# A graph layer: four PSUM banks in one instruction, in place of two and two

## The reference

```python
h = jnp.maximum(_layernorm(x, axis=-1), 0.0)
ea = edge_attr @ W_edge.T + b_edge
msg = jax.nn.relu(h[src] + ea)
aggr = jax.ops.segment_sum(msg, dst, num_segments=N_NODES)
g = (1.0 + eps) * h + aggr
g = jax.nn.relu(g @ W1.T + b1)
x = x + g @ W2.T + b2
```

## Time and profile before

| | |
|---|---|
| median of 3 runs | 1237.12 us (1236.62 to 1238.39) |
| span of the profiled execution | 1239.1 us |
| VectorE busy | 518.5 us, 42% |
| ScalarE busy | 193.0 us, 16% |
| GpSimd busy | 785.9 us, 63% |
| TensorE's matmuls | 628.9 us, 51% |

### The profile page before, as it was taken

How to read it: one execution, slowest core, us unless ns; L and a number is a source line. 1 busy time by engine, 2 the same in 40 slices (tenths; PEclk the granted TensorE clock), 3 DMA queues, 4 the chain that set the end, 5 groups by cost and what they waited for, 6 DMA issues and landing times.

```text
span 1239.1 us, 9124 instructions
## 1 busy us (share of the span) xinstructions
PE 628.9 (51%) x2786; PEld 515.6 (42%) x2786; DVE 518.5 (42%) x658; ACT 193.0 (16%) x233; POOL 785.9 (63%) x838
## 2 busy tenths in 40 slices
PE   2226544455554454555554555444555545554568
PEld 2215434344433334444444444343444434443456
DVE  6645344444433333354344333333343444333373
ACT  5102111111111111111111111111111111111114
POOL 6756666666666666666666666666666666666540
PEclk9999666665656665565665656655556565565668
DMA  8513222333222223333333332222222333232212
GB/s 217 145 33 94 66 64 67 74 85 74 67 67 67 68 67 75 72 73 75 74 93 95 76 74 66 67 67 67 64 66 68 74 88 72 68 67 61 49 29 78
DMA packets 51183, 93.30 MB, mean 75 GB/s; under 512 B 17722, under 2 KB 20443, under 8 KB 51136
## 3 DMA queue, kind: packets, MB, share of 16 engines
q0 software_dynamic: 26592, 40.85, 16.3%
q1 hardware_dynamic: 24390, 51.63, 15.2%
q10 hardware_dynamic: 154, 0.24, 0.1%
HBM read 87.85 MB, written 4.80 MB: 75 GB/s over the span
## 4 chain that ended last, share of the span: by engine, by line
another core or an unknown queue 56%; DVE 23%; issue 8%; DVEq 8%; PE 3%; DMA 1%; ACT 0%; SPq 0%; ACTq 0%
DVE edge_ps L854 7%; DVE edge_ps L865 5%; DVE msg_parts L879 4%; DVEq L768 3%; DVE acc L759 2%; DVEq L770 2%; DVE acc L849 1%; PE edge_ps L601 1%; DVEq L762 1%; DVE stats L639 1%; PE edge_ps L462 1%; DVEq L795 1%; DVE select L705 1%; DVEq L783 1%
## 5 line engine op out<-in xcount | busy, mean ns | idle before, releaser
L352 POOL DMA_INDIRECT gathered<-h_table,src_all x810 | 764.5, 944 | 396.4 <-issue 234.7
L462 PE MATMUL edge_ps<-w_edge,edge_in 97*128 97x96 f32 x1660 | 403.6, 392 | 521.4 <-issue 517.1
L462 PEld LDWEIGHTS edge_ps<-w_edge,edge_in 97*128 97x128 f32 x1660 | 361.8, 302 | 565.0 <-issue 564.1
L787 DVE TENSOR_REDUCE sums<-agg_ps 128x192 f32<-128x576 f32 x41 | 31.0, 757 | 590.4 <-remote 590.4
L424 ACT ACTIVATE msg_parts<-edge_ps 128x960 bf16<-128x960 f32 (+1 forms) x83 | 79.2, 957 | 970.1 <-DVE edge_ps L865 704.4
L543 PE MATMUL agg_ps<-msg_parts,select 128*128 128x288 bf16 x816 | 167.9, 386 | 6.4 <-issue 6.4
L705 DVE TENSOR_TENSOR select<-const_ps,dst_rel 128x2560 bf16<-128x2560 f32 (+1 forms) x43 | 120.8, 2812 | 34.8 <-issue 28.5
L543 PEld LDWEIGHTS agg_ps<-msg_parts,select 128*128 128x128 bf16 x816 | 109.4, 134 | 60.9 <-issue 8.1
L865 DVE TENSOR_TENSOR edge_ps<-edge_ps,gathered 128x960 f32<-128x960 f32 (+1 forms) x83 | 90.9, 1141 | 47.9 <-remote 42.8
L854 DVE SCALAR_TENSOR_TENSOR edge_ps<-edge_ps,msg_parts 128x960 f32<-128x960 f32 (+1 forms) x83 | 91.1, 1144 | 0.3 <-issue 0.3
L879 DVE TENSOR_TENSOR msg_parts<-edge_ps,msg_parts 128x960 bf16<-128x960 f32 (+1 forms) x83 | 90.8, 1136 | 0.3 <-issue 0.3
(11 more groups left out here) (73 smaller groups left out, 143.1 us busy)
## 6 DMA issues: line engine op xcount, KB each, us to landing
edge_in<-edge_t_dram SPq DMA_DIRECT2D x165, 240.0 KB
gathered<-h_table,src_all POOLq DMA_INDIRECT x810
x_all<-x_dram SPq DMA_DIRECT2D x5, 420.0 KB
h_all<-x_dram SPq DMA_DIRECT2D x10, 210.0 KB
out_dram<-h_all SPq DMA_DIRECT2D x10, 210.0 KB
h_table<-h_all SPq DMA_DIRECT2D x3, 420.0 KB
h_table<-h_all SPq DMA_DIRECT2D x1, 630.0 KB
dst_by_row<-dst_rows_dram SPq DMA_DIRECT2D x1, 480.0 KB, 4.2
```

The source lines that it names most:

```text
L352: nc.gpsimd.indirect_dma_start(out=gathered[c % SLOTS][:, at:at + D], out_offset=None, in_=table, in_offset=bass.IndirectOffsetOnAxis(ap=s ...
L462: mm = pe.matmul(edge_bank(c, g)[:, (k - k0) * D:(k - k0 + 1) * D], edge_in[c % SLOTS][:, k * EDGE_TILE:(k + 1) * EDGE_TILE], w_edge[:], s ...
```

## The change

Each of the five steps of the chain is one instruction over a batch of 20 tiles, in place of two over ten tiles each. The two PSUM tensors become one of four banks. A step counts once a batch on its semaphore, so the next step waits for all of it. TensorE waits once, at the head of `edge_features(c)`, for `low_made` of the whole batch before, in place of once for each group of that group's pair. GpSimd waits once a batch for `added`, in place of once a pair. A batch of 16 tiles becomes one piece of 15 tiles and one of 1 (before 10, 5 and 1); batches of 10 and 4 tiles are one instruction as before. LAST uses banks 2 and 3 as before. Line numbers after the change: 848 for 865, 413 for 424, 839 for 854, 417 for 429, 860 for 879, 447 for 462, 344 for 352.

```diff
-        edge_ps = [psum(f"edge_ps{p}", [128, 2 * BANK]) for p in range(PAIRS)]
+        edge_ps = psum("edge_ps", [128, GROUPS * BANK])
...
-        def pieces(c, k0, k1):
-            if k1 - k0 == PAIR_TILES:
-                return [(k0, k1)]
-            return [(g0, g1) for g0, g1 in groups[c] if k0 <= g0 < k1]
+        def pieces(c):
+            whole = tiles_of[c] - tiles_of[c] % GROUP_TILES
+            return [(a, b) for a, b in ((0, whole), (whole, tiles_of[c])) if a < b]
 
         def in_banks(c, k0, k1):
-            if k1 - k0 == PAIR_TILES:
-                banks = edge_ps[k0 // PAIR_TILES][:].rearrange("e (h c) -> e h c", h=2)[:, :, 0:GROUP_TILES * D]
+            h = (k1 - k0) // GROUP_TILES
+            if h:
+                banks = edge_ps[:, 0:h * BANK].rearrange("e (h c) -> e h c", h=h)[:, :, 0:GROUP_TILES * D]
                 return banks.rearrange("e h (t d) -> e h t d", d=D)
...
             for c in range(1, BATCHES):
                 if c >= SLOTS:
                     pool.wait_ge(edge_begun, c)
-                for p, (k0, k1) in enumerate(pairs[c]):
-                    last_use = used_by(c, p, SLOTS)
-                    if last_use is not None:
-                        pool.wait_ge(added, adds_to[last_use] + p + 1)
-                    for k in range(k0, k1):
-                        gather(h_table, c, k)
+                if c >= SLOTS:
+                    pool.wait_ge(added, c - SLOTS + 1)
+                for k in range(tiles_of[c]):
+                    gather(h_table, c, k)
...
             for c in range(LATE):
-                for p, (k0, k1) in enumerate(pairs[c]):
-                    act.wait_ge(added, adds_to[c] + p + 1)
-                    for a, b in pieces(c, k0, k1):
-                        last = nc.scalar.activation(in_parts(msg_parts[c % 2], a, b, 0), in_banks(c, a, b), ACT.Relu)
-                    last.then_inc(high_made, 1)
...
+                act.wait_ge(added, c + 1)
+                for a, b in pieces(c):
+                    last = nc.scalar.activation(in_parts(msg_parts[c % 2], a, b, 0), in_banks(c, a, b), ACT.Relu)
+                last.then_inc(high_made, 1)
...
             def edge_features(c):
+                if c >= 1:
+                    pe.wait_ge(low_made, min(c, LATE))
                 for g, (k0, k1) in enumerate(groups[c]):
                     pe.wait_ge(edges_in[c % SLOTS][g], 16 * loads_to[c][g])
-                    last_use = used_by(c, g // 2, 1)
-                    if c == LAST:
-                        pe.wait_ge(low_made, adds_to[c - 2] + SPARE + 1)
-                    elif last_use is not None:
-                        pe.wait_ge(low_made, adds_to[last_use] + g // 2 + 1)
...
             def take_high(c):
-                for p, (k0, k1) in enumerate(pairs[c]):
-                    dve.wait_ge(high_made, adds_to[c] + p + 1)
-                    for a, b in pieces(c, k0, k1):
-                        last = rest_of(in_banks(c, a, b), in_parts(msg_parts[c % 2], a, b, 0))
-                    last.then_inc(rest_made, 1)
+                dve.wait_ge(high_made, c + 1)
+                for a, b in pieces(c):
+                    last = rest_of(in_banks(c, a, b), in_parts(msg_parts[c % 2], a, b, 0))
+                last.then_inc(rest_made, 1)
```

More of the change, by code:

```diff
@@ L18 @@
 GROUP_TILES = 5
-PAIR_TILES = 2 * GROUP_TILES
 SPLIT = 3
@@ new lines, in add_rows @@
+                for a, b in pieces(c):
+                    put = in_banks(c, a, b) if c < LATE else in_rows(gathered[slot], a, b)
+                    last = nc.vector.tensor_tensor(put, in_banks(c, a, b), in_rows(gathered[slot], a, b), ALU.add)
+                last.then_inc(added, 1)
+            def take_high(c):
+                dve.wait_ge(high_made, c + 1)
+                for a, b in pieces(c):
+                    last = rest_of(in_banks(c, a, b), in_parts(msg_parts[c % 2], a, b, 0))
+                last.then_inc(rest_made, 1)
```

63 lines of the change are left out of this document (25 added, 38 removed).

## The result

| | before | changed |
|---|---|---|
| median, us | 1237.76 (4 runs, 1236.62 to 1238.65) | 1269.33 (4 runs: 1264.00, 1264.59, 1274.07, 1286.00) |
| profiled execution, us | span 1239.1 | 1264.00 (span 1262.2) |
| ratio, 95% interval | | 1.0239 (1.0199 to 1.0279) |

The ratio and its interval leave the run of 1286.00 out. The change makes the kernel slower by 2.4%, or by 26 to 48 us in single runs. I had predicted 5.9 us. Two things stand out already. The four times lie at three levels, 10 to 12 us apart, as if something came two, three or four times. And the spread of the changed kernel is ten times that of before.

A forecast was written before the change was run, and what follows sets the result against it. No engine was near its limit; a batch was taken as tied to its twenty gathers, about 28.5 us. Start 4.6 + batch 0 1.3 + rest 0 = 5.9 us on 1237.1 gave 1243.0 us; own range 1240.5 to 1250, over all 1236.5 to 1256.

The forecast's parts named there:

- The durations and the chain: One batch's five merged steps: 2.16 us each on VectorE, 1.78 on ScalarE, chain 10.33 us, first edge matmul 4.6 us later.
- The first batches: Start of the run, where GpSimd waits for batch 2's edges and nothing covers the chain: +4.6 us.
- Batch 0: GpSimd's burst at 60.99 us, waiting for batch 0's late chain: +1.3 us, bounds 0 to 4.
- The end: Last batches, chain of the 16-tile batch: later sums hidden behind VectorE's own list, 0 us, up to 3.
- The law of the gathers: Steady batches: a batch's time goes with its number of gathers, about 28.5 us for twenty, not with the messages' chain.
- I take 0: Steady batches, 37 distances: edges starting 16.0 us after the first gather stay covered by the 28.5 us, cost 0.
- TensorE may then have more edge matmuls left when its signals come: Steady batches: edge matmuls left over from the later start are absorbed too, as at 98.95 us; cost 0.
- The small price in each batch: Rival: in steady batches the hold ends 0.1 to 0.5 us later, 4 to 19 us in all, 1247 to 1262; chance 0.10.
- The chain as what a batch waits for: Rival: release follows TensorE's start, so each of about 39 batches gains 4.6 us: +180, 1417 us; chance 0.06.

The follow-up runs named there:

- e5: The changed kernel unchanged, run again in the second set beside the kernel before: 1249.98 us, ratio 1.0037.
- e16: The changed kernel unchanged, run again in the fourth set beside the kernel before: 1249.81 us, ratio 1.0029.
- e7: The kernel before, with TensorE waiting once for both halves' low parts in place of once for each half: 1247.30 us, ratio 1.0013.
- e15: The kernel before without GpSimd's wait for edge_begun, run in the fourth set: 1290.86 us, ratio 1.0365.
- third and fifth set: Two groups of follow-up runs, of the changed kernel, the kernel before and variants of both; the kernel before took 1078.61 and 1078.04 us there.
- e1: The kernel before, with a memset of about 4.9 us on VectorE ahead of the add of every batch from 1 on: 1247.91 us, ratio 1.0020.
- e12: The changed kernel unchanged, run again in the third set beside the kernel before: 1084.32 us, ratio 1.0051.

## Why the prediction was wrong, by its own steps

- **The durations and the chain were right.** 2.16 and 1.78 us predicted, 2.16 and 1.77 measured; chain 10.33 predicted, 10.21 measured.
- **The first batches were right.** +4.6 predicted, +4.53 in the first trace, +4.6 to +4.8 in e5 and e16. e7 splits it: 1.3 us for the single wait.
- **Batch 0** came 2.2 us late at 61 us (1.3 predicted), and none of it reached 92.26. This was my lower bound. Where signals are not held, it is the other way about: the 1.3 us are there and the 4.6 are not.
- **The end** was within its bounds (0 to 3) where signals are held, since the way from the last gather to the end scatters from 39.8 to 43.6 us in both kernels. Where they are not held it is above them: 3.4 to 6.4 us between the traces.
- **The law of the gathers** held in every trace of its state, in the ones that break the kernel too: 28.3 to 28.4 us from first gather to signal in e15 but for two batches, and two of them one behind the other in each pair. But it is no law of the kernel. In the third and fifth set it is absent.
- **The step that failed is "I take 0"** for the steady state. I had asked only how late the edges may start, and there I was right (e1 starts them later, and its steady batches cost nothing). I had not asked which of TensorE's signals is released first. `edge_begun` opens the next burst, and nothing sees to it that the hold is over for `edge_done` as well. If it slips through in front of the hold's end, that batch pays the whole chain and half a microsecond. I had put this at 0 for 37 distances; it measured 10.7 us in two of them, and by their times in three and four in the longer runs: 21 to 43 of the 26 to 48 us. I had the clue in hand, in "TensorE may then have more edge matmuls left when its signals come", and called it absorbed because it was so once, at 98.95, where `edge_begun` came at no hold's end at all.
- **The small price in each batch** was the nearest rival (1247 to 1262), with the right place and the wrong form. The price is not 0.1 to 0.5 us in every batch but 10.7 us in two to four of 37.
- **The chain as what a batch waits for** (1417 us) was wrong as a rule for every batch. In a pair it is right, once. The Trainium skill (Perfetto Trace Analysis, Optimizing Scalar/DVE Operations) says that breaking up instructions may let work finish sooner where these engines are not saturated and hold up others. These traces agree at three places: the start (4.5 us), the end where signals are not held (3.4 to 6.4), and each pair (4.5 us dearer merged). In the steady batches it makes no difference.

In the three later sets in which the changed kernel ran, its price was 3.9, 5.7 and 3.6 us (e5, e12, e16), not far from the 5.9 predicted, and in the two with held signals by the mechanism that I had named. In the third set the near hit is luck: the 4.6 us are absent there, and the end, put at 0, pays. The first result was 26 to 48 us. What sets that execution apart is a little visible: its hold is 28.51 us where others have 28.67 to 28.70, and its signals come out early more often. The reduce that ends on `agg_done` usually starts 0.28 us ahead of the next burst. In the kernel before, the reduce of line 787 was up to 1.4 us further ahead there, in the changed kernel the reduce of line 772 up to 4.2 us in batches without a pair. In e5 none is more than 0.1 us ahead, in e16 1.4 at most. Why they differ was not tried. The record names no chip for the first result, and the second and third set show one chip in two states, so a third state of the system is as possible as a different chip.

## What to carry to other kernels

Merging instructions in a chain saves their fixed cost and gives up their overlap. It is free only where the chain is covered, and here it was not covered everywhere: the price stood at the start, or at the end, and in each irregular batch. Look for the event that decides the cover, not for the mean wait: a release that rests on the first instruction of a group, while the consumer needs the last one, can come in front of a hold and turn one late batch into a whole chain. Where a stall fits no instruction of the kernel ("remote", with the producer's rows long done), measure before and after together, on more than one chip and at more than one time, before giving the change its price.

## What the runs showed of the hardware

- TensorE's signals can be held while GpSimd issues indirect gathers: 28.4 to 28.8 us for 20 gathers, 22.8 to 23.1 for 16, 14.5 to 14.7 for 10 in the ordinary batches of the two kernels, with TensorE's rows on a grid of 0.7 us towards the end of a hold. The same kernel took 1246 us on one chip and 1079 us on that chip in a later set, where nothing was held. None of the traces changes from one state to the other in its middle. A trace of the held state has 3,958 to 6,148 semaphore updates, one of the free state 18,037 to 18,244.
- In the held state less work on TensorE costs time: with eight of the twenty matmuls of a batch's sums left out, 1285 us in place of 1246 and 1343 in place of 1250. Where nothing is held it changes nothing (1079 and 1085 us, with and without).
- GpSimd issues a gather every 1.25 us, in bursts of both states. Only in the free state are the batches 25.0 us apart, as that rate gives.
